# Attention in a three-layer kernel: four PSUM banks in the ring of the maxima, and the first group's maxima made during the projection

## The reference

```python
x = x + 0.5 * ffn(layernorm(x), ...)      # shared part + 64 experts, top 6 of them, at most 256 tokens each
x = x + attn(layernorm(x), ...)
x = x + 0.5 * ffn(layernorm(x), ...)
# attn: 16 query heads of 32 channels, one head of keys and values for all
q = (x @ Wq + bq).reshape(b, s, 16, 32).transpose(0, 2, 1, 3)
k = x @ Wk + bk
v = x @ Wv + bv
scores = jnp.einsum('bhsd,btd->bhst', q, k) / sqrt(32)
out = jnp.einsum('bhst,btd->bhsd', softmax(scores), v)
return out.transpose(0, 2, 1, 3).reshape(b, s, 512) @ Wo + bo
```

## Time and profile before

| what | value |
|---|---|
| median of three runs | 3377.15 us |
| profiled execution | 3358.77 us, its span 3357.0 us |
| busy share of the span | PE 87%, VectorE 61%, ScalarE 45%, GpSimd 66% |
| mean granted TensorE clock | 0.927 |
| projection | first load at 621.6 us, last query product at 785.5 us |
| maxima of group 0 | 791.0 to 830.1 us |
| attention proper | 830.2 us to about 2670 us |

### The profile page before, as it was taken

One profiled execution on the slowest core, in us unless ns is written; L12 is line 12 of the kernel. 1 busy time (PEld: TensorE's weight loads), 2 busy tenths in 40 slices (PEclk: granted clock), 3 DMA queues, 4 the chain that ended last, 5 costly groups with the idle time before them and its releaser, 6 DMA issues. The chain is left out here.

```text
span 3357.0 us, 50764 instructions
## 1 busy us (share of the span) xinstructions
PE 2909.1 (87%) x15136; PEld 1560.1 (46%) x15136; DVE 2040.3 (61%) x3891; ACT 1517.1 (45%) x2846; POOL 2206.9 (66%) x1386
## 2 busy tenths in 40 slices
PE   7977777398999999999999999999999889778760
PEld 4644444275444454444444444444444355444430
DVE  7943222476787677677776776776777188322222
ACT  3422222252666565566565655655665444222220
POOL 2158887440888687687787876876877511688870
PEclk9988988697999999999999999999999999888885
DMA  5579999782576667575766666665756343899998
GB/s 212 191 221 242 245 234 227 209 287 92 110 164 133 140 138 144 124 152 118 161 132 128 151 134 141 138 139 125 151 111 149 90 146 120 245 242 233 244 197 310
DMA packets 217009, 576.34 MB, mean 172 GB/s; under 512 B 33948, under 2 KB 34972, under 8 KB 192792
## 3 DMA queue, kind: packets, MB, share of 16 engines
q0 software_dynamic: 84128, 337.69, 50.1%
q1 hardware_dynamic: 128376, 226.84, 20.6%
q10 hardware_dynamic: 4224, 8.39, 0.6%
HBM read 230.94 MB, written 155.24 MB: 115 GB/s over the span
## 5 line engine op out<-in xcount | busy, mean ns | idle before, releaser
L1670 DVE TENSOR_REDUCE attention_mx<-attention_pM 128x1 f32<-128x512 f32 x1984 | 1210.2, 680 | 346.5 <-PE attention_pM L1514 338.5
L1451 ACT ACTIVATE attention_prob<-attention_pS 128x512 f32<-128x512 f32 x2048 | 1060.1, 618 | 609.6 <-PE attention_pS L1501 568.6
L1392 POOL TENSOR_TENSOR attention_pair<-attention_prob 128x1024 f32<-128x1024 f32 x380 | 948.8, 2502 | 269.8 <-ACT attention_prob L1451 265.4
L1514 PE MATMUL attention_pM<-prep_kT,attention_qT 96*128 96x512 f32 x1984 | 877.9, 445 | 0.0
L1501 PE MATMUL attention_pS<-attention_qT,prep_kT 128*128 128x512 f32 x2048 | 841.6, 417 | 24.4 <-issue 17.1
L1501 PEld LDWEIGHTS attention_pS<-attention_qT,prep_kT 128*128 128x128 f32 x2048 | 389.7, 191 | 289.2 <-issue 178.8
L1514 PEld LDWEIGHTS attention_pM<-prep_kT,attention_qT 96*128 96x128 f32 x1984 | 374.2, 190 | 312.0 <-DVE attention_mx L1670 244.3
L1549 PE MATMUL attention_pO<-attention_prob,attention_v 128*32 128x512 f32 x4096 | 492.4, 598 | 0.0
L629 POOL DMA_INDIRECT sum<-experts_res,c_table x256 | 403.3, 1575 | 89.7 <-issue 68.3
L755 DVE TENSOR_SCALAR experts_res<-experts_pD,experts_rows 128x512 f32<-128x512 f32 x128 | 90.8, 746 | 480.0 <-DMA sum<-experts_res,c_table 474.0
L658 PE MATMUL experts_pT<-c_ident,experts_rows 128*128 128x128 f32 x1024 | 184.2, 319 | 188.3 <-DVE experts_xT L739 139.3
(11 more groups left out here) (163 smaller groups left out, 2730.3 us busy)
## 6 DMA issues: line engine op xcount, KB each, us to landing
prep_acc<-attention_pair POOLq DMA_DIRECT2D x96, 1024.0 KB, 7.6
attention_acc<-attention_pair POOLq DMA_DIRECT2D x90, 1024.0 KB, 7.8
experts_wup<-in_L_ffn_w_up_dram SPq DMA_DIRECT2D x128, 256.0 KB, 5.2
attention_qT<-q_parts SPq DMA_DIRECT2D x96, 256.0 KB, 6.6
xn_rows<-route_xn SPq DMA_DIRECT2D x16, 1152.0 KB, 6.3
sum<-route_sh SPq DMA_DIRECT2D x16, 1024.0 KB, 4.4
experts_wdn<-in_L_ffn_w_down_dram SPq DMA_DIRECT2D x64, 256.0 KB, 5.8
attentionp_got<-sum SPq DMA_DIRECT2D x16, 1024.0 KB, 9.1
```

The costliest lines, as they stand in the source:

```text
L1392: pool.tensor_tensor(to[:, part], prob[2 * n % PROBS][:, part], prob[(2 * n + 1) % PROBS][:, part], ALU.add).then_inc(s_pair, 1)
L1451: act.activation(prob[t % PROBS][:, h * QT:(h + 1) * QT], pS[:, at, :], ACT.Exp).then_inc(s_ex, 1)
L1514: pe.matmul(pM[:, r % 3, :], qT[g][0:3 * DH, h, t * P:(t + 1) * P], kT[0:3 * DH, key:key + 512], start=True, stop=True).then_inc(s_mp, 1)
L1670: dve.tensor_reduce(mx[:, unit, part:part + 1], pM[:, r % 3, :], X, ALU.max).then_inc(s_mr, 1)
```

## The change

Three things are changed together.

1. **Ring of four banks.** `pD` is gone and `pM` gets its bank: `RING = 4`, so block r waits for block r-4. The sums over keys of a group (`denominators`) become an item of this ring, behind pair 3. VectorE copies them out (`copy_d`), as its program comes to them, in place of ScalarE after step 10.
2. **First maxima in the projection.** The 64 blocks of group 0 are made in slots 24 to 39 of `project`, four in each slot: two at the slot's start and two at its end, into two new banks (`pF`). Each is reduced by itself.
3. **Adding DMAs.** From turn 2 on, the second input is no longer loaded beside the first and added by VectorE. GpSimd issues a DMA that adds it into the loaded tile (`bring`), six slots and more ahead of its use. The buffers are a ring of six turns, loaded four turns ahead, and two more for the second inputs of turns 0 and 1.

```diff
 def project(...)
-    RING, QB = 4, 4
+    RING, QB, ADDED, LEAD = 6, 4, 2, 4
+    FIRST, SOME = 24, 4
+        pF = m.ps("pF", [P, 2, 512])
+        def first_blocks(s, half):
+            n = SOME * (s - FIRST) + SOME // 2 * half
+            return range(n, n + SOME // 2) if 0 <= n < ahead["items"] else ()
                 def load(i):                                   # SyncE
                     sp.wait_ge(s_xo[i % RING], A + i // RING * 16)
-                    for a in range(2):
-                        sp.dma_start(got[i % RING][a][:, :, :], src).then_inc(s_g[i % RING], 16)
+                    sp.dma_start(got[i % RING][:, :, :], turn_view[0][i, :, :, :]).then_inc(s_g[i % RING], 16)
+                    if i < ADDED:
+                        sp.dma_start(other[i][:, :, :], turn_view[1][i, :, :, :]).then_inc(s_g[i % RING], 16)
-                for i in range(3):
+                for i in range(LEAD):
                     load(i)
+                def bring(i):                                  # GpSimd
+                    pool.wait_ge(s_g[i % RING], A + 16 * loads(i))
+                    pool.sem_inc(k["pool_on"], 1)
+                    pool.dma_start(got[i % RING][:, :, :], turn_view[1][i, :, :, :], accum_op=ALU.add
+                                   ).then_inc(s_on[i % RING], 16)
                 for s in range(SLOTS):
+                    i = (s + 6) // TURN
+                    if (s + 6) % TURN == 0 and ADDED <= i < NTURN:
+                        bring(i)
                     if comes(s - BIAS):
                         output_bias(s - BIAS)
+                def first_maxima(n):                           # TensorE
+                    if n == 0:
+                        pe.wait_ge(ahead["in"], A + 48)
+                        pe.wait_ge(s_kl, A + CHUNKS // 2)
+                    pe.wait_ge(ahead["reduced"], A + n - 1)
+                    pe.matmul(pF[:, n % 2, :], ahead["q"][0:3 * DH, h, t * P:(t + 1) * P],
+                              kT[0:3 * DH, part * 512:(part + 1) * 512], start=True, stop=True
+                              ).then_inc(ahead["made"], 1)
                 for s in range(SLOTS):
+                    for n in first_blocks(s, 0):
+                        first_maxima(n)
                     ...
+                    for n in first_blocks(s, 1):
+                        first_maxima(n)
+                def first_maxima(n):                           # VectorE; placed in its slots in the same way
+                    dve.wait_ge(ahead["made"], A + n + 1)
+                    dve.tensor_reduce(ahead["mx"][:, n:n + 1], pF[:, n % 2, :], X, ALU.max).then_inc(ahead["reduced"], 1)
 def attention(...)
-        COPY_STEP = 10
+        RING = 4
-        pD = m.ps("pD", [P, QT])
-        pM = m.ps("pM", [P, 3, 512])
+        pM = m.ps("pM", [P, RING, 512])
                 def copy_d(G):                                 # ScalarE
-                    act.wait_ge(s_sum, A + (G + 1) * 2)
-                    act.wait_ge(s_do, A + 64 * G)
-                    act.activation(d_sb[:, :], pD[:, :], ACT.Copy).then_inc(s_dc, 1)
                 def maxima(base, r, n, g, batch, G):           # TensorE
-                    pe.wait_ge(s_mr, A + base + max(r - 2, 0))
+                    pe.wait_ge(s_mr, A + base + max(r - RING + 1, 0))
+                def denominators(base, r, c, g):
+                    pe.wait_ge(s_mr, A + base + max(r - RING + 1, 0))
+                    for n in range(2):
+                        pe.wait_ge(s_acc[g % 2][n], (c * 2 + (g // 2 + 1)) * (3 * 16))
+                        for h in range(HG):
+                            ins = pe.matmul(pM[h * DH:(h + 1) * DH, r % RING, :], k["ones32"][:, :],
+                                            acc[g % 2][n][:, h * QT:(h + 1) * QT], start=n == 0, stop=n == 1)
+                    ins.then_inc(s_mp, 1)
                         if p == SUM_PAIR and not first:
-                            denominators(c, g - 1, 0)
-                            denominators(c, g - 1, 1)
+                            denominators(base, r, c if g else c - 1, (g - 1) % GPC)
+                            r += 1
-                pe.wait_ge(s_q[0], A + 48)
-                for n in range(ITEMS):
-                    first_maxima(n)
+                def copy_d(base, r, G):                        # VectorE, behind pair 3
+                    dve.wait_ge(s_mp, A + base + r + 1)
+                    dve.wait_ge(s_do, A + 64 * G)
+                    dve.tensor_copy(d_sb[:, :], pM[:, r % RING, :]).then_inc(s_dc, 1)
+                    dve.wait_ge(s_dc, A + G + 1)
+                    dve.sem_inc(s_mr, 1)
-                for n in range(0, ITEMS, 3):
-                    ...
-                    dve.tensor_reduce(flat[:, n:n + some], bank[:, 0:some, :], X, ALU.max).then_inc(s_fr, 1)
```

More of the change, by code:

```diff
@@ L952, in project @@
         SLOTS = NT + PARTS
+        turn_view = [part[0:N, :].rearrange("(i t p) c -> i p t c", t=TURN, p=P) for part in sums]
         with nc.Block() as block:
@@ L1023, in _ @@
             def _(pe):
-                begin(pe, s_tr, s_pq, s_pv, s_pk)
+                begin(pe, s_tr, s_pq, s_pv, s_pk, ahead["made"])
                 def transposes(t, j):
@@ L1168, in _ @@
                             values(i)
+                    for n in first_blocks(s, 1):
+                        first_maxima(n)
+                dve.wait_ge(ahead["reduced"], A + ahead["items"])
                 dve.wait_ge(s_kl, A + NTURN)
@@ L1206, in attention @@
         ITEMS = UNITS * BLOCKS
+        mx = m.sb("mx", [P, UNITS, BLOCKS])
+        project(nc, tag + "p", k, prep, q_d, kT, v_sb, sums, xb_d, {
+            "queries": first_queries,
+            "q": qT[0],
+            "in": s_q[0],
+            "mx": mx[:, :, :].rearrange("p u b -> p (u b)"),
+            "items": ITEMS,
+            "made": m.sem("fp"),
+            "reduced": m.sem("fr"),
+        })
+        PROBS = 4
+        HALF = HG * QT // 2
         PAIRS = STEPS // 2
+        RING = 4
         EARLY = 2
@@ L1253, in attention @@
         s_acc = [m.sems(f"acc{b}", 2) for b in range(2)]
[L1254 removed]
+        s_lsum = m.sem("lsum")
         s_dc = m.sem("dc")
@@ L1470, in body @@
                                 exponential(G, t, h)
-                            if t == COPY_STEP and not first:
-                                copy_d(G - 1)
                         if not (g == GPC - 1 and isinstance(c, int) and c == CHUNKS - 1):
@@ L1725, in group @@
                             r += 1
+                        if p == SUM_PAIR and not first:
+                            copy_d(base, r, G - 1)
+                            r += 1
                         if p == RECIPROCAL_PAIR and not first:
```

118 lines of the change are left out of this document (51 added, 67 removed).

## The result

| what | before | after |
|---|---|---|
| median of four runs each | 3375.08 us (3371.05 to 3379.41) | 3288.32 us (3284.79 to 3292.36) |
| ratio, 95% interval | | 0.9742 (0.9731 to 0.9753) |
| first load to first shifts | 208.9 us | 201.2 us |
| first to last shifts (31 groups) | 1768.2 us | 1687.7 us |
| before the first load / behind the last shifts | 621.6 / 758.3 us | 631.5 / 766.6 us |

"Shifts" is the start of VectorE's last step of `make_shifts` (L1685 before, L1731 after); the time of a group is counted from one such step to the next. The change gives 7.7 + 80.5 = 88 us by these two rows, and 87 us by the medians. The two profiled executions differ by only 70 us, since the untouched stages took 9.8 and 8.3 us longer in the second one. That belongs to the execution: a profile of the same kernel on another chip has its first load at 622.33 us and 757.7 us behind its last shifts.

The account below looks back on a forecast made before the run. TensorE's order of work was taken to set attention's pace, with blocks waiting for VectorE in a three-bank ring. Ring -75.6, ScalarE's copy -0.5 and projection -4.6 made about -81 us on 3377: 3296 us, 8 in 10 for 3267 to 3335.

Parts of the forecast that it names:

- Ring, pair and head: Attention: a fourth bank removes 0.30 us of waiting a pair and 0.60 us a head; -75.6 us over 31 groups.
- pairs 1 to 5: Attention: five pairs of a group win 0.30 us each; with 0.60 at its start, a group wins 2.1 us.
- Group 1 of a chunk: Attention groups with output products: pairs 1, 2, 4 and 6 win about 0.60 us each, 3.6 us a group in all.
- The first group: Where attention begins: the clock would be at its lower level as before, so no difference.
- Pair 6 and the sums: Attention: pair 6 wins 0; VectorE's copy of the sums delays pair 4's reductions up to 0.3 us, cost 0, no slack.
- The -0.5 us for ScalarE's last copy: Last group: ScalarE loses 31 copies of about 0.5 us, hidden behind TensorE except the last, so -0.5 us.
- The stretch of first maxima: Behind the projection: VectorE's program from 790.96 to 830.17 goes, except a memset of 0.48; -38.7 us.
- Blocks in slots: Projection: four blocks side by side cost TensorE 2.0 us, 0.93 work and 1.07 waiting; +31 us, bounds +15 and +45.
- Adding DMAs, start: Projection start: GpSimd's first adding DMA waits for turn 2's load, landing at about 637.0, and delays tile 1; +3.5 us.
- The sign of being wrong: Projection: moments waiting for an adding DMA would show the forecast wrong; adding loads starving the projection had 5%.
- The stall of the stores: Fifth projection turn: ScalarE's 7.07 us wait for a query store; taken as -1 us, between -7 and +10.
- The clock: Projection slots 24 to 39: rival that TensorE's pauses lower the clock, 3376 us, no change; 6%.

Follow-up runs that it names:

- ring only: Kernel before with only the changed attention (four banks, VectorE copying the sums); projection, its loads and first maxima as before: ratio 0.9760.
- plain loads: Changed kernel, but SyncE loads both inputs of every turn and VectorE adds them, no adding DMA: ratio 0.9729 to the kernel before.
- adds, no blocks: Changed kernel, but group 0's maxima are made in a stretch of their own behind the projection; adding DMAs stay: ratio 0.9761 to the kernel before.
- waits of three banks: Changed kernel with its four banks, but a block waits as if there were three: ratio 0.9982 to the kernel before.
- plain loads, spread: Changed kernel, but VectorE adds plainly loaded inputs, and each slot's second two blocks stand amid the query products: ratio 0.9700 to the kernel before.

## Why the prediction was right

**Ring, pair and head: the mechanism holds, and its waits to 0.02 us; the size was small.** Forecast -75.6 us, measured -80.5 (-80 to -84 over all profiles with the ring). A pair won its 0.30 us of waiting; the term "pairs 1 to 5" missed that the values behind the last block also start 0.1 us sooner once that block does not wait: five pairs, 0.5 us a group, 2.6 in place of 2.1, over 24 groups 12 us. The head won 0.58 (forecast 0.60). Of these 12 us under 6 are in the sum: the first group won 1.4 us, several won 2.2 to 2.5, and two groups in which TensorE also sits idle for some 5.5 to 6 us that the rows put down to "issue" won 1.0 and 0.8. In the second profile of the same kernel those two won 2.4 and 2.9, which is the difference between its 1684.4 us and 1687.7. Group 1 of a chunk won 3.4 to 3.6 (3.6), but not as worked out: the outputs behind pairs 1, 2 and 6 won 0.6 each, pairs 3 and 5 won 0.4 and not 0.3, and pair 4, behind the copy, won 0.4 and not 0.6.

**The first group.** "No difference" was too simple: it won 1.4 us, not 2.6. New in its rows is the wait of 1.18 us for the output weights, and the clock is at the lower level for nearly all of 832 to 842 us (0.50 and 0.52 in its two halves), where it was 0.50 and then 0.72 in 830 to 840 before. But with the ring only, which has no such wait, it won 1.6, so the shares of the two stay open.

**Pair 6 and the sums.** As worked out: no gain at the tail, and in plain groups no cost at the copy (0.69 + 0.15 us). The fear that there is no slack was right: with one bank of lead less the same copy costs 0.2 to 0.3 us a group. The -0.5 us for ScalarE's last copy can't be seen, as the time behind the last shifts is 755 to 767 us over the profiles.

**The stretch of first maxima.** -39.2 against -38.7 forecast; it is the plain distance of two rows of the kernel before.

**Blocks in slots.** 2.12 us per four against 2.0, +33.7 (as the rest) against +31.6.

**Adding DMAs, start.** +5.4 against +3.5; against the three profiles with plain loads and their starts of 30.9 to 32.0 us it is up to 6.7. The place and the queue were right. The load was expected at 637.0, 15.4 us behind the first; GpSimd was released 17.0 us behind it (648.42 less 631.46). In 15.6 us the queues had moved 336 GB/s x 15.6 us = 5.24 MB, the size of five loads, but the load of turn 3 is among the loads in the queue and can have taken its share; I had counted five loads alone. No experiment tests this. The sign of being wrong that I had named, moments that wait for an adding DMA, did not come, so these loads don't starve the projection: at 307 GB/s the share of 1.03 (forecast 1.0) still lets a turn of 16.2 us through.

**The stall of the stores: wrong.** I took -1 us, between -7 and +10, and 7.6 went. The step that failed is the sum over edits: the stall was priced against the loads alone. The loads gave 3.1 to 3.7 us of it, and the blocks, priced at their full 2.0 us in the slots of that turn, hid the rest, since a stage that is held up in one place does not add what it waits for in another. The stall was also taken for a wait alone: 2.9 of its 7.6 us were the lower clock behind the wait, which went with it.

**The clock.** It stayed at 1.00 in the slots of the changed kernel, where the second two blocks wait 0.55 us each time; the old stretch of first maxima had run at 0.50. That stretch was no case of a cold start: the clock was at 1.00 until 790.0 us, TensorE stood idle from 785.9 to 791.0, and the clock fell in this pause. With plain loads it fell twice, each time behind a wait for a bank (2.54 and 1.00 us). The Trainium skill's rule of psum-queue depth-cycling ("TensorE: Matmul & The Clock Gate", section "A second HAM failure mode: psum-queue depth-cycling") has the clock of such a kernel swing between its two levels; that does not show in the changed kernel, and the two falls with plain loads agree with it. Banks are not needed for it, however: in the kernel before and in *adds, no blocks* it fell behind waits of 4.62 and 2.26 us for ScalarE. Nor does the length of one wait tell: with plain loads and the blocks spread it stayed at 1.00 over waits of 1.28 us. When it falls stays open.

**The sum.** The missed terms add up to -5 us in the ring and -3 in the projection. The latter is luck in part: the blocks and the start cost 4 us more than forecast, and the stall gave 6.6 more. The forecast of 3296 us stood on a median of 3377.15 us, and the median of the kernel before is now 3375.08; that is 2 of the 8 us between forecast and result.

## What to carry to other kernels

- Count the banks of a PSUM ring against the consumer's pace within one burst, not over the loop: VectorE was busy 74% and still held TensorE, as it is slower than TensorE for the length of eight blocks. One more bank, found by making a rarely used one an item of the ring, took 80 us off; the same bank with the blocks' old wait took nothing off.
- Work put into the gaps of another stage costs its waits too. Place it by twos where its consumer has time between them; four side by side into two banks cost more than twice their work (2.12 us for 0.93).
- A DMA whose issue has to wait for another stops everything behind it on the issuing engine. Issue it when its load has landed.
- Look at the clock behind a stall. A wait of 4.62 us cost the kernel before 7.6 us, and 2.9 of these were the work done at the lower level behind it.

## What the runs showed of the hardware

- Behind a block that had waited for its bank, the matmuls with the values started 0.42 to 0.44 us after it; behind one that had not, 0.32. The rows of three kernels (before, changed, waits of three banks) have it so; what in TensorE makes it is open.
- TensorE's clock was at the lower level for 3.4 to 6.8 us behind waits of 4.62 (before), 2.26 (adds, no blocks), 2.54 and 1.00 us (plain loads), and stayed at the upper one over 0.55 us in every slot (changed) and over 1.28 us (plain loads, spread).
- The same 307 to 308 GB/s of the projection cost a DMA share of 1.03 with adding DMAs and 0.87 with plain ones.
- One execution's untouched stages can be 18 us off another's on a program of one core. Differences of profiles were therefore taken between marks around the change.
